# Six images instead of eight beside the edge sort, and 24 more row gathers ahead of the segments

## The reference, cut to what matters

```python
edge_index = jax.random.randint(ks[6], (2, N_EDGES), 0, B * N, jnp.int32)   # B, N = (16, 1024)
...
s = relu(einsum('bcp,bcq->bpq', xn, xn)) ** 2          # per image, 2304 x 2304
x = x + einsum('bpq,bcq->bcp', s, g)
t = to_tokens(x);  h = (layernorm(t) @ W_gat)           # one row per node
e = leaky_relu(a_src[src] + a_dst[dst])                 # per edge
alpha = exp(e - segment_max(e, dst)) / segment_sum(...)
agg = segment_sum(h[src] * alpha, dst)                  # then layernorm, top 2 of 4 experts
out = sum over experts of gate * (gelu(t @ W1 + b1) @ W2 + b2)
```

## Time and profile before

| | us |
|---|---|
| median of 3 runs | 5309.23 (5308.4 to 5329.4) |
| the profiled execution, its own time | 5277.24 |
| its span | 5275.0 |
| PE, DVE, ACT, POOL busy | 3485.0, 3971.9, 3404.4, 2951.8 |
| indirect gathers L980 | 2048, busy 2125.1 |

### The profile page before, as it was taken

The page is one execution under the profiler, slowest core; times in us unless marked ns, Lnnn a source line. Parts: engine busy times, 40 slices in busy tenths (PEclk is TensorE's granted clock), DMA queues, the critical chain, the costliest instruction groups (busy, mean ns, idle before and its releaser), DMA issues.

```text
span 5275.0 us, 70367 instructions
## 1 busy us (share of the span) xinstructions
PE 3485.0 (66%) x22687; PEld 1462.8 (28%) x22687; DVE 3971.9 (75%) x5512; ACT 3404.4 (65%) x4010; POOL 2951.8 (56%) x2937
## 2 busy tenths in 40 slices
PE   4888988500499999999999999900000017777777
PEld 1223333200244444444444444400000002222222
DVE  8998988997677777777776656606778948778777
ACT  4777988400677777778777787704445626666666
POOL 6000000048777777777777777777774147666661
PEclk9999999755699999999999999955555558898899
DMA  6100100002122222222222222224445526999997
GB/s 259 36 20 20 31 23 16 17 14 83 22 48 58 54 55 55 55 56 50 55 59 52 58 49 53 48 46 143 158 150 194 169 72 137 152 157 158 159 157 151
DMA packets 332471, 441.87 MB, mean 84 GB/s; under 512 B 183193, under 2 KB 261916, under 8 KB 331500
## 3 DMA queue, kind: packets, MB, share of 16 engines
q1 hardware_dynamic: 209744, 288.12, 19.1%
q0 software_dynamic: 105536, 148.61, 16.7%
q10 hardware_dynamic: 16896, 1.18, 0.3%
HBM read 252.35 MB, written 166.47 MB: 79 GB/s over the span
## 4 chain that ended last, share of the span: by engine, by line
POOL 39%; issue 14%; DMA 13%; DVE 8%; PE 3%; ACT 2%; SPq 1%; ACTq 0%; POOLq 0%; DVEq 0%
POOL rows L980 35%; DMA rows<-htab_d,idx 7%; DMA gs<-gates_d 5%; POOL R L1759 2%; PE ye L1931 1%; PE up L1943 1%; DVE S L2508 1%; DVE AD L2493 1%; DVE AE L2487 1%; DVE ms L2630 1%; POOL nb L1716 1%; DMA gates_d<-GH 1%; POOL got L1714 1%; ACT hid L2155 1%; ACT L2155 0%
## 5 line engine op out<-in xcount | busy, mean ns | idle before, releaser
L980 POOL DMA_INDIRECT rows<-htab_d,idx x2048 | 2125.1, 1038 | 668.0 <-issue 594.1
L2063 ACT ACTIVATE rel<-gram 128x1024 f32<-128x1024 f32 (+1 forms) x1080 | 1003.0, 933 | 337.3 <-PE gram L1875 331.5
L2408 DVE SCALAR_TENSOR_TENSOR s<-gram,rel 128x1024 f32<-128x1024 f32 (+1 forms) x720 | 792.6, 1116 | 557.9 <-ACT rel L2063 541.7
L1829 PE MATMUL acc<-s,gT 128*64 128x512 f32 (+1 forms) x4320 | 1028.3, 553 | 0.5 <-issue 0.4
L1875 PE MATMUL gram<-hl 128*64 128x512 f16 (+1 forms) x4320 | 794.3, 365 | 102.4 <-DVE s L2408 59.9
L1875 PE MATMUL gram<-hl,lh 128*64 128x512 f16 (+1 forms) x4320 | 784.6, 361 | 0.0
L1759 POOL DMA_INDIRECT R<-seg_d,nidx x576 | 577.7, 1003 | 195.1 <-issue 169.6
L1080 POOL IOTA slots<- 64x2048 int32 x1 | 1.8, 1833 | 975.5 <-POOLq L192 975.5
L1931 PE MATMUL ye<-hid,w 128*64 128x384 f32 x1536 | 365.9, 555 | 267.9 <-DVE ms L2630 188.9
L1914 PE MATMUL tailsT<-ident,tails 128*20 128x128 f32 x24 | 5.3, 415 | 793.6 <-DVE tails L2516 793.6
L2155 ACT ACTIVATE hid<-up,b1t 128x768 f32<-128x768 f32 x384 | 335.6, 899 | 277.4 <-PE up L1943 266.7
(11 more groups left out here) (372 smaller groups left out, 5429.4 us busy)
## 6 DMA issues: line engine op xcount, KB each, us to landing
gs<-gates_d SPq DMA_DIRECT2D x64, 1024.0 KB, 16.7
rows<-htab_d,idx POOLq DMA_INDIRECT x2048
seg_d<-state SPq DMA_DIRECT2D x32, 996.0 KB, 4.4
raw_d<-w_zeros POOLq DMA_DIRECT2D x48, 512.0 KB, 23.3
raw_d<-rows POOLq DMA_DIRECT2D x32, 768.0 KB, 3.6
tne<-tn_d SPq DMA_DIRECT2D x32, 576.0 KB
x2e<-x_d SPq DMA_DIRECT2D x32, 576.0 KB
out<-res SPq DMA_DIRECT2D x64, 256.0 KB
```

Source lines behind the costliest of these rows:

```text
L980: pool.indirect_dma_start(out=n.rows[:, k % 2, j, :], out_offset=None, in_=n.htabx, in_offset=bass.IndirectOffsetOnAxis(ap=n.idx[:, g % 2, ...
L1829: last = pe.matmul(acc[(par + c) % 2][j * C:(j + 1) * C, 0:w], gT[:, par, 2 * k + j, :], s2[:, u % SLOTS, j * w:(j + 1) * w], start=k == 0 ...
L2063: act.activation(rel[:, t % RELS, 0:2 * w].rearrange("p (j x) -> p j x", j=2), gram[(par + t) % 2][:, :, 0:w], ACT.Relu, scale=1.0 / SPLIT ...
L2408: dve.scalar_tensor_tensor(halves(s2[:, t % SLOTS, 0:2 * w]), gram[(par + t) % 2][:, :, 0:w], 1.0 / SPLIT ** 2, halves(rel[:, t % RELS, 0: ...
```

## The change

`FIRST` becomes 6, so that images 6 and 7 leave the sort and become the first two of `walk`, which now has 26 images. The count `t` up to which GpSimd gathers before it waits for `img_done` becomes 28 * 64 + 24 = 1816 in place of 1792.

```diff
-FIRST = 8
+FIRST = 6
...
     AHEAD = 28
+    OVER = 24
...
-            t = AHEAD * GC
+            t = AHEAD * GC + OVER
             gather_rows(pool, n, OPENING, t)
             pool.wait_ge(img_done, 1)
```

## The result

The changed kernel takes 5684.7 us (median of 5 runs, 5682.8 to 5694.0) against 5309.9 us (median of 5 runs now, where the table above has 3): a ratio of 1.070 (1.068 to 1.073), 375 us slower.

What follows compares the result with a forecast made beforehand. GpSimd's gathers were taken to bound the kernel from the sort's end to mid-segments. First segment step +392 us, segment stage -9, sum +383 on the median 5309: 5692 us, 7.2% more; four-in-five range 5645 to 5740.

Steps and rivals of the forecast that it cites:

- The mechanism: GpSimd's wait for `o_hx`: the first gather stands until image 7's rows are stored, so gathers start 442 us later.
- The rivals: First chunks don't need images 6 and 7 (+6 us, 4%); images pace the sort (4%); gathers run free (3%).
- pace the sort: Sort: PE and ACT hold it back, so two fewer images save 232 us; +193, 5502 us; chance 4%.
- run free: Walk: 1816 gathers at 1.25 us each beside the images, ending at 3838; +266, 5575 us; chance 3%.
- The starting time: First gather at 1568 instead of 1126: image 7 landed at 1618, less 42 us (sort) and 8 (merge and routes).
- The term for the routes: Merge and routes: predicated copies speed up without gathers beside them, 8 us taken, 13 at most, nothing at least.
- The collision of the earlier trace: Merge and routes: a gather issued at 1250.3 took 6.39 us beside a 5.62 us scan, against 0.94 alone.
- The made-up part: Walk and after: 1508 gathers out before `img_done` at 3570, 308 alone for 385 us; first segment step +392 us.
- The segment stage: Segments: 24 fewer gathers there take 43 us off, DVE's pace gives back 34; 9 us shorter, bounds 0 and 43.
- Behind the segments: After the segments: nothing changes in count or order, so no time was added.

Runs made afterwards that it cites:

- six_again: The changed kernel run again, unaltered, beside the kernel before: 5649.7 us, ratio 1.072 to the kernel before.
- six_over0: The changed kernel with OVER = 0 in place of 24, so 1792 gathers ahead of the segments: 5622.3 us, ratio 1.067 to the kernel before.
- eight_over24: The kernel before with FIRST = 8 kept and 1816 gathers ahead of the segments in place of 1792: 5295.2 us, ratio 1.004.
- eight_near: The kernel before with gathered row numbers cut off at 13824, so need falls from 128 to 96: 5270.2 us, ratio 0.999.

## Why the prediction was right, point by point

**The mechanism was right and shown.** The step on which all rests, that the first gather waits for image 7, is shown by the wait of 495.7 us in the trace, by its release by the second store of the walk, and by the two kernels that need fewer images: with seven the loss shrinks by 76 us, with six it is gone. The rivals are out. The images do not pace the sort: it ended 51 us earlier, not 232. The gathers did not run free: 1.33 us beside the `level` images and 1.305 beside the plain ones (1248/938, 745/571), where I had 1.342 and 1.304.

**The starting time was right by two errors that cancel.** I had -42 us for the sort and -8 for merge and routes, and the first gather at 1568; it is at 1568.1, which is luck. The sort took all of it. The merge starts at 1021.8 in place of 1072.6, 51 us earlier, and merge and routes take the same time as before. Of the 51 us, DVE's work is 35.4 (932.2 in the earlier trace rows less 896.8), near the 36.8 worked out; its idle time fell by 15.6 us, not 5. The line for the whole sort (PE, PEld, DVE, ACT, POOL):

```profile
66.00:1021.00 955.00, 621.84 (x3148) 244.91 (x3148) 896.83 (x567) 583.00 (x782) 29.65 (x63) 0.84 0.12 42
```

The idle time went mainly at three places: the wait for PE's sums from 10.4 to 4.3 us, the wait for ACT's exchanges from 42.0 to 37.4, the one for `w_sd` ahead of L391 from 3.4 to 0.4. I had taken the second as not image work; it shrank all the same when two images left.

**The term for the routes was wrong.** I read the mean of the predicated copies above their median as a cost of the gathers beside them. Without a gather there, the same copies have the same mean, 1496 ns, and a median of 1302 against 1298 (DVE by line and form, 1050 to 1350; to be read against the earlier trace rows):

```profile
L2204 DVE COPY_PREDICATED edges<-mrow,edges 128x1024 f32<-128x1024 uint8 x11 | 16.5, 1496 | 19.5 <-ACT edges L2029 19.2
```

DVE's busy time in the 275 us is 227.8 us in both kernels. The spread lies in the eleven copies themselves. They exchange neighbouring runs of 1, 2, 4 elements and so on, doubling from copy to copy; in the changed kernel, without a gather beside them, the first two (runs of 1 and 2) take 2.43 and 2.44 us and the other nine 1.25 to 1.32. The second and the third:

```profile
1254.43 2.44 DVE L2204 COPY_PREDICATED edges<-mrow,edges 128x1024 f32<-128x1024 uint8 x1
...
1261.87 1.25 DVE L2204 COPY_PREDICATED edges<-mrow,edges 128x1024 f32<-128x1024 uint8 x1
```

The collision of the earlier trace rows has one victim, GpSimd: the scan takes 5.62 us in the changed kernel too (L2224), with no gather beside it. What held that gather is less plain than I put it. It ended at 1256.7, 1.9 us after the scan and 0.1 us after the `TENSOR_SCALAR` that ran from 1255.07 to 1256.60 (L2225), so the trace doesn't tell the two apart.

**The made-up part was right.** 930 + 578 gathers were expected before `img_done`, 938 + 571 are there; behind it 308 alone for 385 us were expected, and there are 309 in 390 us, 1.26 us each. `img_done` came at 3561.6 rather than 3570, because the two further images took 160 us (3561.6 - 3452.5 + 51), not 167. The first segment read is at 3951 against 3955: I had `img_done` 8 us too late and the gathers behind it 5 us too short, which nearly cancel.

**The segment stage** should have been shorter by 9 us. From the first to the last scan it is 661.2 us against 662.5 in this pair, 655.9 against 665.4 with six images (`six_again` and `six_over0`, on two chips), and 657.0 with `eight_over24`. The pairs give 1 to 10 us, and the profiles, one for each kernel, don't settle it better. The mechanism is there: 18 steps take longer than 20 us, where 20 did.

**Behind the segments** I added nothing. The last read of the segments is 387 us later (4586.1 against 4199.5), and the span 407 us longer; the 20 us between them lie in the expert part, of which before and after have the same instructions. They don't belong to the change: from the last read to the end it is 1096 us in this profile and 1076 in that of before, but 1075 in `six_again`, which is the same changed kernel, and 1066 to 1081 in all ten experiments. What lengthened that one execution stays open. Up to the last read the profiles differ by 387 us, against a sum of 383, and the medians by 375. I had put the sum on the median of before, and not on its profile: 5692 against 5684.7. On the profile it would have been 5660 against 5683.9; no run shows why the profiled execution of before was 32 us below its median, so the closer of the two is partly luck.

## What to carry to other kernels

Ahead of moving work out of a stretch, look at what waits for its last result by data, and where that result comes afterwards: here a semaphore that had always been open became a wait of 496 us for the engine that bounds the kernel, while the stretch that got lighter gave back 51. Slack has to be used from the side that waits: the images were early by 111 us and the gathers late, so fewer gathers ahead helped by 45 us and more of them cost 23. A mean above its median is no sign of contention until the same instructions have been seen without the neighbour.

## What the runs showed of the hardware that was not expected

Contention between VectorE and GpSimd was one-sided in this stretch. GpSimd's transfers beside merge and routes took 1.69 us each instead of 1.25, but VectorE's instructions there were as long with 162 gathers beside them as with none (211 instructions, 227.76 and 227.78 us busy). Rows that repeat (16% of the gathered rows in `eight_near` are one row) changed the price of a gather beside the images by less than 1% (1248/933 = 1.338 against 1.342, 587/454 = 1.293 against 1.304). Copies of one shape, 128x1024, took 2.43 and 2.44 us with runs of 1 and 2 elements and 1.25 to 1.32 us with longer ones.
